# A four-layer residual stack on one core: the SSM's products spread over steps 0 to 3 and 5, its output formed in one operation, Wo kept per batch half

## The reference, cut to what matters

```
x = x + RNN(x)      # h = tanh(x_t Wx + b + h Wh), 1024 steps in sequence
x = x + SSM(x)      # conv over 4 taps (taps from the condition), then
                    #   B_t = softplus(conv Wp_B + bp), C_t = tanh(conv Wp_C + bp), u_t = x Ws + bs
                    #   state = decay * state + dt * B_t * u_t       (64 states)
                    #   y_t = C_t * state;   out = y Wo + bo
x = x + LSTM(x)     # 4 gates, hidden size 512, 1024 steps in sequence
x = x + x @ layer_n # one 512 x 512 matrix per batch element, from a small network
```

## Time and profile before

| | |
|---|---|
| Profiled execution | 3902.44 us, its span 3900.6 us |
| Instructions in the span | 255332 |
| TensorE busy (matmul) | 3628.1 us, 93% |
| TensorE busy (weight loads) | 3055.5 us, 78% |
| VectorE busy | 3253.3 us, 83% |
| ScalarE busy | 1648.2 us, 42% |
| GpSimd busy | 774.8 us, 20% |
| Mean DMA rate | 16 GB/s |

### The profile page before, as it was taken

How to read it: one execution, slowest core, us unless ns; L and a number is a source line. 1 busy time by engine, 2 the same in 40 slices (tenths; PEclk the granted TensorE clock), 3 DMA queues, 4 the chain that set the end, 5 groups by cost and what they waited for, 6 DMA issues and landing times.

```text
span 3900.6 us, 255332 instructions
## 1 busy us (share of the span) xinstructions
PE 3628.1 (93%) x110596; PEld 3055.5 (78%) x110596; DVE 3253.3 (83%) x19153; ACT 1648.2 (42%) x8244; POOL 774.8 (20%) x3623
## 2 busy tenths in 40 slices
PE   7899999999999999999999999999999999999875
PEld 4688788888888888888888888888888888877754
DVE  6688888888888888888888888888888888888766
ACT  4244444444444444444444444444444444444332
POOL 0122222222222222222222222222222222212111
PEclk9999999999999999999999999999999999999999
DMA  7100000000000000000000000000000000000000
GB/s 277 49 7 7 10 10 10 7 9 8 10 10 10 10 7 7 10 10 10 10 7 7 9 10 10 10 8 9 7 10 10 10 10 7 7 7 7 7 6 8
DMA packets 19109, 63.32 MB, mean 16 GB/s; under 512 B 3958, under 2 KB 4526, under 8 KB 14914
## 3 DMA queue, kind: packets, MB, share of 16 engines
q1 hardware_dynamic: 17692, 46.67, 3.7%
q10 hardware_dynamic: 294, 0.33, 0.0%
HBM read 38.48 MB, written 8.39 MB: 12 GB/s over the span
## 4 chain that ended last, share of the span: by engine, by line
DVE 50%; PE 44%; issue 4%; DMA 1%; ACT 1%; ACTq 0%; DVEq 0%; SPq 0%; POOL 0%; POOLq 0%
PE ps_lstm L1040 34%; DVE lstm_sums L745 18%; DVE ps_lstm L750 8%; DVE lstm_ig_fc L756 5%; DVE rnn_sums L854 5%; DVE lstm_gates_2c L761 5%; DVE lstm_h_parts L785 3%; PE ps_rnn L1079 3%; PE ps_ssm L1121 2%; DVE lstm_h_scaled L778 2%; DVE lstm_h_parts L781 2%; PE ps_lstm_in_b L1121 2%; PE ps_lstm_in_a L1184 1%; DMA layer_plus_2I<-in_L_cond_w 1%; DVE rnn_h_parts L869 1%
## 5 line engine op out<-in xcount | busy, mean ns | idle before, releaser
L1040 PE MATMUL ps_lstm<-lstm_Wh_parts,lstm_h_parts 128*20 128x256 f16 x65472 | 1975.0, 273 | 228.2 <-DVE lstm_h_parts L785 149.2
L1040 PEld LDWEIGHTS ps_lstm<-lstm_Wh_parts,lstm_h_parts 128*20 128x20 f16 x65472 | 1547.1, 91 | 629.3 <-DVE lstm_h_parts L785 472.4
L745 DVE STREAM_TRANSPOSE lstm_sums<-ps_lstm 128x256 f32<-128x256 f32 x2048 | 912.9, 446 | 202.9 <-PE ps_lstm L1040 175.3
L487 ACT ACTIVATE lstm_gates_2c<-ps_lstm 128x32 f32<-128x32 f32 x2048 | 403.9, 197 | 1419.4 <-DVE ps_lstm L750 1419.4
L351 POOL COPY lstm_sums<-lstm_in 128x32 f32<-128x32 f32 x2048 | 423.8, 210 | 1747.4 <-DVE ps_lstm L750 1747.4
L1079 PE MATMUL ps_rnn<-rnn_Wh_parts,rnn_h_parts 128*20 128x128 f16 x32736 | 636.9, 219 | 24.0 <-DVE rnn_h_parts L869 22.6
L1079 PEld LDWEIGHTS ps_rnn<-rnn_Wh_parts,rnn_h_parts 128*20 128x20 f16 x32736 | 545.5, 92 | 63.9 <-DVE rnn_h_parts L869 47.0
L750 DVE TENSOR_REDUCE ps_lstm<-lstm_sums 128x32 f32<-128x96 f32 x2048 | 554.9, 271 | 34.2
L496 ACT ACTIVATE lstm_tanh_c<-lstm_gates_2c 128x8 f32<-128x8 f32 x2048 | 419.3, 205 | 254.1 <-DVE lstm_gates_2c L761 254.1
L781 DVE TENSOR_TENSOR lstm_h_parts<-lstm_o_scaled,lstm_tanh_c 128x8 f16<-128x8 f32 x2048 | 334.1, 163 | 129.3 <-ACT lstm_tanh_c L496 42.8
L492 ACT ACTIVATE lstm_o_scaled<-lstm_gates_2c 128x8 f32<-128x8 f32 x2048 | 427.4, 209 | 32.1
(11 more groups left out here) (186 smaller groups left out, 2661.8 us busy)
## 6 DMA issues: line engine op xcount, KB each, us to landing
layer_plus_2I<-in_L_cond_w SPq DMA_DIRECT2D x16, 1024.0 KB, 6.4
out<-out_rows SPq DMA_DIRECT2D x128, 64.0 KB, 1.6
x_rows<-in_x SPq DMA_DIRECT2D x31, 256.0 KB
lstm_Wx<-in_L_cond_Wh SPq DMA_DIRECT2D x1, 4096.0 KB, 17.7
lstm_Wx<-in_L_cond_Wx SPq DMA_DIRECT2D x1, 4096.0 KB, 13.9
layer_plus_2I<-in_L_cond_Wh SPq DMA_DIRECT2D x1, 1024.0 KB, 9.0
rnn_Wx<-in_L_cond_Wx SPq DMA_DIRECT2D x1, 1024.0 KB, 11.4
lstm_in<-in_L_cond_w SPq DMA_DIRECT2D x1, 1024.0 KB, 10.3
```

The costliest lines, as they stand in the source:

```text
L745: return mark(V.transpose(tr[h][s % 2][:, :, 0:QC], psL[h][:, 0:HW].rearrange("p (g c) -> p g c", c=QC)))
L1040: ins = mm(psL[h][QC * j:QC * j + LO + NB, 0:HW], hls[:, k, :], whl[:, k, h, e, j, :], start=(k == 0 and e == 0), stop=(k == KB - 1 and e ...
```

## The change

The SSM's 36 products stand 8 each in steps 0 to 3 and 4 in step 5, in place of 9 each in steps 0 to 3; ScalarE's tanh for C_t moves from step 5 to 6. The last layer's product of step 5 moves behind the others: its four fourths are now in steps 11, 28, 29 and 30, and the hold products of step 30 are gone.

`y` becomes 128 partitions by 64 columns, written by one operation; it no longer has a zero part. In place of it Wo is stored per batch half: `wo_pad[:, h, :]` holds Wo in partitions 64h to 64h+63 and zero elsewhere. The product with Wo becomes 4 x 2 products, each of 64 columns, into every second pair of columns of the PSUM tile. POOL clears `wo_pad` instead of `y`, and SP waits for that before it loads Wo.

VectorE's waits for the filled x of both halves of step 0 stand at the head of the chunk, ahead of the RNN's hi part.

```diff
-OUT_STEPS = [5, 11, 28, 29]
+OUT_STEPS = [11, 28, 29, 30]
-SSM_CUTS = [0, 9, 18, 27, 36]
+SSM_CUTS = [0, 8, 16, 24, 32, 32, 36]
-CT_STEP = 5
+CT_STEP = 6
-HOLD_STEPS = [30, 31]
+HOLD_STEPS = [31]
...
-        wo2 = stage[:, 10 * 512:11 * 512]
-        y = stage[:, 11 * 512:11 * 512 + TOK].rearrange("p (t n) -> p t n", n=NB)
+        y = stage[:, 11 * 512:11 * 512 + HS]
+        wo_pad = sb("ssm_Wo_by_half", [P, 2, D])
...
+            sp.wait_ge(q_id, 3)
             for h in range(2):
-                sp.dma_start(wo2[NS * h:NS * (h + 1), :], Wo[:, :]).then_inc(d_ssm, 16)
+                sp.dma_start(wo_pad[NS * h:NS * (h + 1), h, :], Wo[:, :]).then_inc(d_ssm, 16)
...
-            nc.gpsimd.memset(y, 0.0).then_inc(q_id, 1)
+            nc.gpsimd.memset(wo_pad[:, :, :], 0.0).then_inc(q_id, 1)
...
                 def transpose(h, s):
-                    if s == 0:
-                        vec.wait_ge(S[f"lstm_in_ready{h}"], 1)
                     vec.wait_ge(S[f"lstm_mm{h}"], s + 1)
...
-                        for h in range(2):
-                            own = slice(NS * h, NS * (h + 1))
-                            V.scalar_tensor_tensor(out=y[own, :, 2 * h:2 * h + 2], in0=states[own], scalar=spt[own, 1:2],
-                                                   in1=ct.rearrange("p (t n) -> p t n", n=2)[own], op0=ALU.mult, op1=ALU.mult
-                                                   ).then_inc(S["y_ready"], 1)
+                        V.scalar_tensor_tensor(out=y, in0=st_, scalar=spt[:, 1:2], in1=ct, op0=ALU.mult, op1=ALU.mult
+                                               ).then_inc(S["y_ready"], 1)
...
                 carried = w["rnn"] and p["lstm"]
+                if w["lstm"]:
+                    for h in range(NH):
+                        vec.wait_ge(S[f"lstm_in_ready{h}"], 1)
                 if carried:
                     rnn_hi(S_last, CT - 1)
...
-                        pe.wait_ge(S["y_ready"], 2)
+                        pe.wait_ge(S["y_ready"], 1)
                         for b in range(KB):
-                            last = mm(psX[:, TOK * b:TOK * (b + 1)], wo2[:, P * b:P * (b + 1)], y.rearrange("p t n -> p (t n)"),
-                                      start=False, stop=(b == KB - 1))
+                            o_ = psX[:, TOK * b:TOK * (b + 1)].rearrange("p (t n) -> p t n", n=NB)
+                            for h in range(2):
+                                last = mm(o_[:, :, 2 * h:2 * h + 2], wo_pad[:, h, P * b:P * (b + 1)],
+                                          y.rearrange("p (t n) -> p t n", n=2), start=False, stop=(b == KB - 1 and h == 1))
```

More of the change, by code:

```diff
@@ L828, in ssm_stage @@
                         mark(V.tensor_copy(st0[:, :], states[:, CT - 1, :]))
-                        if known == 1:
-                            vec.wait_ge(q_id, 3)
-                        for h in range(2):
-                            own = slice(NS * h, NS * (h + 1))
-                            V.scalar_tensor_tensor(out=y[own, :, 2 * h:2 * h + 2], in0=states[own], scalar=spt[own, 1:2],
-                                                   in1=ct.rearrange("p (t n) -> p t n", n=2)[own], op0=ALU.mult, op1=ALU.mult
-                                                   ).then_inc(S["y_ready"], 1)
+                        V.scalar_tensor_tensor(out=y, in0=st_, scalar=spt[:, 1:2], in1=ct, op0=ALU.mult, op1=ALU.mult
+                                               ).then_inc(S["y_ready"], 1)
                 def series(out_, in_, c, x_):
```

## The result

The changed kernel took 3915.86 us (median of 7 runs, 3911.01 to 3918.59), the kernel before beside it 3904.04: a ratio of 1.003, interval 1.002 to 1.0039. It is slower by about 12 us. The forecast was 3919.2, "slower".

What follows compares the result with a forecast made beforehand. One loop alternating between VectorE (50%) and TensorE (44%) was taken to bound the kernel. Terms 22.5 - 2.0 - 2.5 - 1.2 = +16.8 on the profiled 3902.44 gave 3919.2 us; the sum's own range was 3912.9 to 3927.1.

Steps and rivals of the forecast that it cites:

- Wo by halves: Step 9's Wo products: eight added records at 0.11 us cost 0.89, 0.72 late per full chunk; sum +22.5 us.
- iteration 1: Chunk 1, with only the RNN's short loop and little room: Wo products cost +0.7 us.
- rival (1): The stream sets the Wo products' pace, so steps 8 and 9 gain: 3892.2 us; chance 0.10.
- (2): Rival: load and stream of the Wo products don't overlap, +1.83 us before room: 3946.5 us; chance 0.03.
- Iteration 32: Chunk 32, which lacks the RNN products and so has room: Wo products cost +0.2 us.
- The y operation: Step 8: one operation for two saves VectorE 0.29 to 0.37 and the step's 0.12 excess, but counts 0 in the sum.
- Step 0: One SSM product less returns the step to 3.59 us: 29 x 0.07 = -2.0 us.
- Steps 1 to 3: More room per step takes back part of TensorE's 7.9 us of issue stalls: -2.5 us, bounds 0 and 7.9.
- Rival (4): All issue stalls go: 3913.8 us; chance 0.83 together with the forecast.
- The heads: Chunk heads: moving the x waits off the first transposition gains 0.07 at 18 heads, -1.2 us; bounds -2.1 and +3.
- two more waits push it by as much as they save: Heads where the loop branches back: the waits delay the RNN's hi part as much as they save, so no gain.
- Rival (3): Head waits hold the hi and lo parts and RNN products 0.2 too long, +6.2 us: 3926.6 us; chance 0.04.

Runs made afterwards that it cites:

- the kernel with half the columns: Changed kernel with each Wo product streaming 32 columns instead of 64, adding the SSM's output for only the first half of each chunk: 3913.57 us.
- the cuts alone: Kernel before with only TensorE's order changed (SSM products 8, 8, 8, 8, 0, 4; tanh, out and hold steps moved): 3892.57 us, ratio 0.9975.
- the Wo edit alone: Kernel before with Wo per batch half, y as one operation and eight Wo products, nothing else: 3922.03 us, ratio 1.0051.
- 64-wide form: Changed kernel with each Wo tile cut into two 64-wide column halves side by side, 16 products for 8: 3913.68 us, ratio 1.0039.

## Why the prediction came out

**Wo by halves: right, in mechanism and in size.** The forecast's 0.72 us a chunk for steps 8 and 9 together came as 8.07 less 7.34, 0.73; over the kernel it is +22.0, and +22.7 with iteration 1, for +22.5. The choice made in it, that a record with a 128-wide fp32 load costs 0.11 whatever it streams, is what the kernel with half the columns shows, and rival (1), the stream's pace, falls with it; so does (2), load and stream added, which asked for 2.7 us. Iteration 32 was close (+0.25 for 0.2), and iteration 1 paid the 0.7 put down for it (an RNN step of 2.71 for 2.01).

**The y operation: right.** It takes 0.28, and step 8 lost its 0.12. As said, that isn't to be added: the pair paid the 0.72.

**Step 0: right** (-2.5 for -2.0); the cuts alone give it. Of the 2.5 some 1.7 are the 0.06 a chunk that was forecast; the rest is one stall that went (0.6) and the first chunk.

**Steps 1 to 3: the term that was mis-sized.** Taken at -2.5 with a bound of -7.9, it was -7.7. The reason given, more room in the step, isn't it: the Wo edit alone, with the old cuts, clears them as well. Nor did the 7.9 us of issue rows measure them, as these fell by 4.7. The stalls stand where TensorE's records, counted from the branch, reach 7680 and 7936. In before these are the 54th and the 46th of the 72 records of a step's SSM products, behind which TensorE is late; in after and with the cuts alone they fall among LSTM products. With the Wo edit alone they are the 38th and the 30th, and cost nothing, which is not explained. What share the smaller slices have of their own stays open, since every version with new cuts also has other work at these two records. Rival (4), all stalls go, was the nearer: 3913.8 for a measured 3915.86.

**The heads: the step "two more waits push it by as much as they save" failed.** The hi part was pushed by 0.1, and that did not cancel the 0.07: with the overlap taken away the branch head gains 0.05 (3.62 for 3.66). It was made twice as long by GpSimd's addition, which starts when the fills end, as the hi part now does. The forecast looked for what the wait holds up and not for what runs beside the waiting instruction once it is released. Plain heads gained the 0.07 put down for them (3.66 to 3.59), branch heads lost 0.15. Sum +0.8 for -1.2. Rival (3), heads that hold up the RNN by 0.2 in each chunk, would have cost 7.4 more and isn't seen.

**Entry and exit of the loop: not in the forecast**, -2.6. These three steps take 5.1 to 7.7 us each in every kernel without the longer loop, and differ between kernels by up to 2.6 with no edit near them. (With the longer loop the step across the last head of the loop takes 3.59.)

The misses outside Wo sum to some -8, in the spans 8.5 for the 16.8 forecast. That is below the lower end of the sum's own range, +10.5, as the profiled 3911.01 is below 3912.9. The median of after lies 4.8 above its profiled run, so that 3915.9 stands nearer to 3919.2 than the sum's parts deserve: half of the agreement is the spread of the runs.

## What to carry to other kernels

Count TensorE's small fp32 products by their weight loads: splitting a product to stream less doubles the loads, and where these set the pace the split costs its full number of records. Before paying, ask what the split frees (here 0.12 us of VectorE for 0.84 of TensorE); the rest of this change, without it, beats both kernels (0.9981). When a wait is moved, look at what its releaser starts next on its own engine, since the released instruction will run beside it; and measure a version's parts together, as a longer loop body can cost more than the edit gives.

## What the runs showed of the hardware

**VectorE beside GpSimd.** The hi part, a 128x16 TENSOR_SCALAR, takes 0.15 to 0.18 alone or beside GpSimd's 128x16 copies in the kernel before. Beside a 128x64 addition that began 0.03 us ahead of it, it takes 0.31 to 0.33 (some 310 times), beside one that began with it or up to 0.12 behind 0.17 to 0.19 (some 40 times). At the branch heads of after, where the addition begins 0.02 behind it, it takes 0.37; at the plain heads, where the last 128x32 copy begins with it, 0.24. In after, VectorE and then GpSimd:

```profile
1452.47 0.32 DVE L858 TENSOR_SCALAR rnn_h_parts<-rnn_h 128x16 f16<-128x16 f32 x1 [0.17 <-ACT rnn_h L511]
```

```profile
1452.44 0.32 POOL L378 TENSOR_TENSOR x_scaled<-x_scaled,lstm_h_scaled 128x64 f32<-128x64 f32 x1
```

The Trainium skill (SBUF — State Buffer, section "Who interferes with whom") says that VectorE and GpSimd take a shared pair of ports as an exclusive lock, a tensor_scalar among those that can. The additions are in line with it; the 128x16 copies, which don't slow the hi part, are not what the rule alone would have one expect.

**The branch back.** With TensorE's loop longer by eight hold products, or by as many records in 64-wide form, its first products behind the branch come 3.6 to 4.2 us after the last transposition instead of 2.27, and the steps across heads lose 21 us in the one and 14 in the other. The branch instruction takes 2.5 to 3.1 us instead of 0.35 to 0.44, with a 16 KiB packet of instructions under way, the 55th of the pass. 54 packets a pass go with 13765 to 13821 TensorE records, 55 with 13861; 54 times 256 is 13824. A length between was not tried, nor one above.

**Every 256 records.** TensorE's stalls in dense SSM products stand at multiples of 256 records behind the branch, at 7680 and 7936 above all, and cost 0.1 to 0.6 us each. 128 satisfied waits ahead of the loop leave them there; the sum over steps 1 to 3 differs by +4.2 us in the kernel before and by +3.0 in the 64-wide form, on one trace each. On this kernel a difference of 4 us between versions is no evidence for an edit by itself.
